# Attention slots: the order in which ScalarE and VectorE read TensorE's banks

## The reference, cut to what matters

```python
qkv = x @ w_qkv                                   # 32 query heads, 8 key/value heads, 16 wide
xq, xk = _apply_rope(xq), _apply_rope(xk)
scores = jnp.einsum('bhsd,bhtd->bhst', xq, keys) * scale
scores = jnp.where(causal, scores, -jnp.inf)
probs = jax.nn.softmax(scores, axis=-1)
out = jnp.einsum('bhst,bhtd->bhsd', probs, values)
return out @ w_o
```

## Time and profile before

| | us |
|---|---|
| median of 3 runs | 1969.58 |
| runs | 1962.2 to 1971.93 |
| the profiled execution | 1970.87 |
| its span, first to last instruction | 1968.9 |
| TensorE busy in the span | 1709.1 (87%) |
| VectorE, ScalarE, GpSimd busy | 1033.5, 792.3, 600.0 |
| mean granted TensorE clock | 0.938 of 2.4 GHz |

### The profile page before, as it was taken

One profiled execution on the slowest core, in us unless ns is written; L12 is line 12 of the kernel. 1 busy time (PEld: TensorE's weight loads), 2 busy tenths in 40 slices (PEclk: granted clock), 3 DMA queues, 4 the chain that ended last, 5 costly groups with the idle time before them and its releaser, 6 DMA issues. The chain is left out here.

```text
span 1968.9 us, 26012 instructions
## 1 busy us (share of the span) xinstructions
PE 1709.1 (87%) x9045; PEld 1436.7 (73%) x9045; DVE 1033.5 (52%) x2013; ACT 792.3 (40%) x1595; POOL 600.0 (30%) x792
## 2 busy tenths in 40 slices
PE   6898898699999999999999999306998899899884
PEld 5887887588888888777878888204787777777773
DVE  6666645552223223674243324592767767767772
ACT  3555445222212221222121211233877776776760
POOL 4344425121111111432111114305343543543422
PEclk9888888699999999999999999757999999999996
DMA  4000000200001101321010101200000000000000
GB/s 130 12 12 22 1 1 1 70 27 22 24 21 33 32 23 30 115 68 50 17 43 28 38 1 43 95 0 0 1 1 12 6 7 12 11 2 12 12 6 17
DMA packets 28548, 52.16 MB, mean 26 GB/s; under 512 B 3520, under 2 KB 4704, under 8 KB 28416
## 3 DMA queue, kind: packets, MB, share of 16 engines
q1 hardware_dynamic: 28416, 50.47, 8.3%
HBM read 42.07 MB, written 8.39 MB: 26 GB/s over the span
## 5 line engine op out<-in xcount | busy, mean ns | idle before, releaser
L1149 POOL TENSOR_TENSOR m_a_lo<-m_prod,m_a_hi 128x512 fp32r<-128x512 f32 x100 | 130.8, 1308 | 640.8 <-ACT m_a_hi L1207 640.8
L114 PE MATMUL m_ps<-m_hT_hi,m_w_hi 128*128 128x512 f32 x800 | 317.8, 397 | 8.4 <-DVE m_w_lo L1305 5.3
L1323 DVE TENSOR_TENSOR m_prod<-m_prod,m_ps 128x512 f32<-128x512 f32 x100 | 68.7, 687 | 481.7 <-ACT m_prod L1203 481.6
L116 PE MATMUL m_ps<-m_hT_hi,m_w_lo 128*128 128x512 f32 x800 | 317.7, 397 | 0.0
L115 PE MATMUL m_ps<-m_hT_lo,m_w_hi 128*128 128x512 f32 x800 | 316.9, 396 | 0.0
L1203 ACT ACTIVATE m_prod<-m_ps 128x512 f32<-128x512 f32 x100 | 59.7, 597 | 577.3 <-PE m_ps L116 577.3
L1780 ACT ACTIVATE t_p<-t_ps,t_nmax 128x128 f32<-128x128 f32 (+1 forms) x512 | 181.5, 425 | 74.7 <-DVE t_nmax L1902 74.5
L114 PEld LDWEIGHTS m_ps<-m_hT_hi,m_w_hi 128*128 128x128 f32 x800 | 151.2, 189 | 45.0 <-issue 5.7
L1902 DVE TENSOR_REDUCE t_nmax<-t_ps 128x2 f32<-128x512 f32 (+1 forms) x192 | 131.9, 687 | 96.7 <-PE t_ps L1971 60.1
L115 PEld LDWEIGHTS m_ps<-m_hT_lo,m_w_hi 128*128 128x128 f32 x800 | 151.2, 189 | 36.4
L116 PEld LDWEIGHTS m_ps<-m_hT_hi,m_w_lo 128*128 128x128 f32 x800 | 151.0, 189 | 36.5
(11 more groups left out here) (257 smaller groups left out, 3808.4 us busy)
## 6 DMA issues: line engine op xcount, KB each, us to landing
m_raw<-in_w_mlp SPq DMA_DIRECT2D x75, 256.0 KB, 2.7
a_xt<-in_x SPq DMA_DIRECT2D x8, 512.0 KB, 3.7
m_old<-in_x SPq DMA_DIRECT2D x16, 256.0 KB, 3.1
x_store<-stream SPq DMA_DIRECT2D x4, 1024.0 KB, 5.2
m_old<-x_store SPq DMA_DIRECT2D x16, 256.0 KB, 2.7
out<-t_yl SPq DMA_DIRECT2D x16, 256.0 KB, 2.0
q_raw<-in_w_attn SPq DMA_DIRECT2D x10, 256.0 KB, 5.4
a_att<-in_w_mixer SPq DMA_DIRECT2D x8, 256.0 KB, 2.8
```

The lines of the kernel that those rows point to most:

```text
L114: pe.matmul(out, w_hi, x_hi, start=first, stop=False)
L116: return pe.matmul(out, w_lo, x_hi, start=False, stop=last)
L1149: pool.tensor_tensor(a_lo[:, n % 2, :], prod[:, :], f(a_hi[:, n % 2, :]), ALU.subtract).then_inc(lo, 1)
L1323: dve.tensor_tensor(prod[:, :], prod[:, :], ps[:, U + TURN_AT["unit", n, 0] % 2, :], ALU.mult).then_inc(prodd, 1)
```

## The change

In every slot, ScalarE takes the high part of the turned probabilities before its drain, not after it. VectorE takes the low part first, then the maximum, and only then the drain and `turned_low`. Nothing else is changed: TensorE's and GpSimd's programs, the job table and all waits stay.

```diff
@@ ScalarE @@
             for s in range(FIRST_SLOT, END_SLOT):
                 b, n = s // UNITS, s % UNITS
+                if 0 <= s - 1 < SLOTS:
+                    high(s - 1)
                 drain(s)
                 if n in (0, 2) and in_batch(b - 1):
                     values_out(2, n // 2, b - 1)
...
-                if 0 <= s - 1 < SLOTS:
-                    high(s - 1)
                 if 0 <= s + 1 < SLOTS:
                     exponentials(s + 1)
@@ VectorE @@
             for s in range(FIRST_SLOT, END_SLOT):
                 b, n = s // UNITS, s % UNITS
-                drain(s)
+                if 0 <= s - 1 < SLOTS:
+                    low(s - 1)
                 if 0 <= s + 1 < SLOTS:
                     maximum(s + 1)
+                drain(s)
                 turned_low(s)
-                if 0 <= s - 1 < SLOTS:
-                    low(s - 1)
```

## The result

| | before | after |
|---|---|---|
| median, us | 1966.78 (4 runs) | 2158.26 (4 runs) |
| runs, us | 1962.2 to 1971.93 | 2155.58 to 2167.61 |
| profiled execution, us (span) | 1970.87 (1968.9) | 2167.61 (2165.5) |
| mean granted TensorE clock | 0.938 | 0.910 |

The changed kernel takes 1.098 of the time of before (95% interval 1.094 to 1.102), some 191 us more. 2109 had been forecast, with a range of 2050 to 2180. The execution that was profiled is the longest of its kernel; the other three had a mean clock of 0.917 to 0.919. A fifth run, not in the table, took 2160.99 us at 0.916.

A forecast was written before the change was run, and what follows sets the result against it. TensorE was taken as close to bound in the attention stage (446.8 of 500 us busy). Late reads cost 16.7 us a batch, 100 us over six, plus 23 and 16 for first and last: 139 together, so 2109 us, range 2050 to 2180.

The forecast's parts named there:

- The steps of slot 9: Slot 9: high part ends 0.64, low from 0.66, maximum 1.26, query read 1.86 to 3.21, TensorE on at 3.26: 2.6 us.
- the sum: Attention stage, slot by slot: TensorE's delays from late bank reads, adding to 16.7 us in each full batch.
- the likeliest case: Attention stage: TensorE keeps full clock and only late reads cost, 139 us in all, 2109 us; chance 0.62.
- granted clock 1.0: Sign that the forecast is right: TensorE's granted clock stays at 1.0 in the attention stage.
- The second case: Rival, attention stage: TensorE's clock falls as well, 41 us more, 2150 us (2190 with two falls a batch); chance 0.24.
- so this hides: VectorE's maximum comes 0.8 us late each slot, but its exponentials are wanted a slot later, so no cost.
- The terms of which only a sum was given: Losses in the other slots (1 to 4, 13 to 20, 22), estimated from read times, 6.45 us a batch.
- the ends of the stage: First and last batches, lacking some jobs: 23 us and 16 us more.
- the ceiling of 31 us: Upper limit for the estimated 6.45 us term: slot 9's 2.6 us in each of twelve slots.
- only the reads already waited for would move: Rival: only slots 7, 10, 19 and 22 pay, some 1 us each, 32 us, 2001 us; chance 0.09.
- The other side: Rival: the low part was the bottleneck, displaced reads fit behind it; gain at most 14 us, 1956 us; chance 0.03.
- It doesn't do what it says: Rival: where ScalarE is late already, high part and drain merely swap; no change, 1970 us; chance 0.02.

The follow-up runs named there:

- the run with fillers: Changed kernel plus 3 to 10 extra 128x512 mask matmuls into a free bank ahead of the jobs of ten slots: 2115.78 us, ratio to before 1.076.
- the run with six slots: Kernel before, with the changed order on both engines only in slots 8, 11, 12, 16, 18 and 23 of each batch: 1987.35 us, ratio 1.010.

## Why the prediction was right, and where it fell short

**The direction and the mechanism** hold. The steps of slot 9 came within 0.01 us of the times of the sum. With the clock out of the way (the run with fillers), the terms stand against the sum, in us over before:

| slots | sum | with fillers | after |
|---|---|---|---|
| 5 | 2.5 | 2.60 | 3.98 |
| 9 | 2.6 | 2.70 | 3.95 |
| 10 | 1.5 | 1.54 | 2.03 |
| 21 | 1.9 | 2.00 | 2.00 |
| 6 and 7 | 1.7 | 1.89 | 2.38 |
| 1, 2, 3, 4 | 3.6 | 3.75 | 3.67 |
| 13, 14 to 17 | 1.3 | 1.60 | 1.56 |
| 18 and 19 | 0.4 | 0.59 | 1.86 |
| 20, 22 | 1.15 | 1.36 | 2.13 |
| 0, 8, 11, 12, 23 | 0 | 0.47 | 1.24 |
| batch | 16.7 | 18.4 | 24.8 |

The row of 18 and 19 is a difference of larger terms: with fillers slot 18 is 1.6 us shorter and slot 19 2.2 longer, which the sum did not show.

The six full batches gave 110.6 us with fillers (100 in the sum) and 148.7 after. The first batch lost 20.9 (23 in the sum), the last 21.3 (16); 4.8 us passed before the first slot and 0.9 after the last. Together that is the 196.6 us by which the two profiled spans differ. The 4.8 us can't be put down to the change: with fillers the order is the same, and the first slot ends 2.7 us earlier than before the change, so that part varies from one execution to the next by as much.

**The step that failed is the clock.** The forecast took full clock in the attention stage as the likeliest case (0.62 against 0.24) and named "granted clock 1.0" as a sign. It was 0.92. The second case, with its 2150, is what happened: the measured 2158 lies 49 us over the forecast and 8 over that case. That its price came so near is luck. It was put at 8 to 16 falls in the stage of at most 5.1 us each, so 41 to 82 us. Measured (the changed kernel less the one with fillers) it is 42.5 us, but from 33 falls of some 1.3 us each: about four times the falls at a quarter of the price. 95.6 of the 582 us of the six batches ran at 1.2 GHz, in 24 stretches of 3.4 us and two of 6.8, which began in slots 5, 7, 9, 10, 19 and 22; the mixer's in the earlier trace rows was 10.2.

Against the case I had set that the stage kept 2.4 GHz with a tenth of its time idle. That is a mean over slots. TensorE's longest wait there was 1.8 us, and one of some 1.5 us came in each batch, in slot 22; the change made waits of 2.3 to 2.8 us, on average, in each of slots 5, 7, 9, 19 and 22. The mixer's row, 1.59 busy of 3.42 us, was the nearer witness (it ends 2.4 us before the fall; the 3.4 us right before it show 1.55), and slot 9's 0.82 of 3.27 lies beyond it. The length of one wait does not settle it: with the maximum put first, waits of 1.6 us came in slots 5 and 9 of every batch and the clock stayed at 1.00, while with ScalarE's order alone it fell in slot 7 of four of the six batches and not in that of the other two, with a wait of 0.8 us and one of 1.3 in all six. Where the limit lies is open.

The Trainium skill says, on the page "TensorE: Matmul & The Clock Gate" (section "A second HAM failure mode: psum-queue depth-cycling"), that frequent short idle times between groups of matmuls, with PSUM banks used in turn, made one kernel's clock swing. The trace of before has banks in turn and 84 waits over 0.25 us in the stage, and shows no fall, so by itself that was not enough here; the changed kernel shows the swing, 33 falls in the stage. With fillers the jobs take their banks in the same turns, and the clock stays at 1.00, so the cause is the time that TensorE idles, not the use of the banks.

Of the other signs, the waits for `t_qk`, `t_yl` and `t_osum` are new and that of L2004 is nearly gone, as said; the gap in slot 9 is 2.45 us (2.3 expected). TensorE's busy time per batch did not stay: 73.3 us in place of 64.7, since matmuls at 1.2 GHz last longer.

**A smaller step that failed**: "so this hides", of the late maximum. It hides from the transposes, but ScalarE's exponentials then stand ahead of its drain in the *next* slot. In the run with six slots this costs 0.2 to 0.6 us in slots 1, 17 and 19, and a maximum that is later still costs 0.5 to 0.8 more in slots 1, 3, 12 and 15. Slots 8, 11, 12 and 23 were put at nothing; with fillers they cost 0.4, in slot 12, where the drain of `o` was overlooked (wanted at 1.01, free at 1.34).

**The terms of which only a sum was given** (6.45) came out at 7.3 with fillers, and the ends of the stage (39) at 35.5 with fillers and 42 after: off by 13% and 9%, where up to half had been allowed for. Two slips in the working change nothing in the result: half of both terms is 39 us, so the likeliest case by itself went from 2070 to 2148, not 2060 to 2140; and the ceiling of 31 us counts twelve slots where thirteen are listed (34 us).

**The rivals.** That only the reads already waited for would move (2001 us) falls with slots 5 and 9, where 24.0 us of new waits stand in the 500 us. The other side (1956 us) was right in one thing: the wait for `t_pT_lo` went from 10.7 to 1.4 us; what it was worth, at most 14 us, was lost over ten times. "It doesn't do what it says" falls too.

Left open is how the clock's cost divides over the slots of the changed kernel, since it is read as a difference of two kernels, and how far fillers delay jobs. In slot 9 they end at 1749.60, before the job starts, but slot 1 is 0.1 us longer with them than without. Whatever they delay makes the run with fillers longer than a changed kernel at full clock would be, so the clock's 42.5 us are a floor rather than a ceiling.

## What to carry to other kernels

Order an engine's queue by when its input is ready and when its output is asked for, not by which result seems most urgent: an instruction that must wait for this step's work holds back every read behind it, and the cost is the time from when the matrix engine asks for the bank to the end of the displaced read. A read put off can pay twice, since the gap can also bring the matrix engine's clock down, as it did here; judge that from the slots with the longest waits, not from the mean busy share. And where two engines feed each other, moving one half of a pair can be worse than moving both, so test the halves.

## What the runs showed that I had not expected

Filling TensorE's waits with 71 matmuls a batch whose results are thrown away made the changed kernel 42.5 us faster, with clock 1.00 in place of 0.92 between 1400 and 1900 us. At 1.2 GHz a 128x256 matmul started 0.21 us after the last, against 0.12 at 2.4 GHz. Moving VectorE's half alone cost 256 us over before, the whole change 191, ScalarE's half alone 39.
